# The end of a two-layer transformer kernel: first half's int8 product made with rows on partitions, scaled by ScalarE and transposed home; the last two tiles one by one; residual adds on GpSimd; four stores

## The chip, the cores and the metric

One Trainium2 chip; the kernel runs on one of its cores. The metric is the device time of one execution in microseconds, as the median of several runs. The engines are named as the profile names them: PE is TensorE (matmuls), DVE is VectorE, ACT is ScalarE, POOL is GpSimd, and SP issues most of the DMAs. PE writes into PSUM, which has eight banks here (`bank0` to `bank7`, each 128 partitions by 512 float32); POOL works on SBUF alone in this kernel.

## What is computed

Two pre-normalised transformer layers over `x` of shape (2, 512, 256), float32. Only the last block, the int8 layer of layer 1, is touched by the change:

```python
x = x + _L0_attn_ref(_layernorm(x), ...)
x = x + _L0_ffn_ref(_layernorm(x), ...)
x = x + _L1_attn_ref(_layernorm(x), ...)
x = x + _L1_ffn_ref(_layernorm(x), weight, bias)

def _L1_ffn_ref(x, weight, bias):
    w_scale = clip(max(abs(weight), axis=1), 1e-8) / 127
    w_q = clip(round(weight / w_scale), -128, 127)          # one scale per output row
    x_scale = maximum(max(abs(x), axis=2) / 127, 1e-12)     # one scale per token
    x_q = clip(round(x / x_scale), -128, 127)
    acc = einsum('bnd,od->bno', x_q, w_q)
    return acc * x_scale * w_scale + bias
```

## The kernel before

The 1024 tokens are eight tiles of 128 tokens (tokens on partitions, 256 features in the free dimension); tiles 0 to 3 are the first half, 4 to 7 the second. `X[:, t, :]` holds the residual stream of tile t. Every engine has its own instruction list, written out by hand, and the lists meet at semaphores. The attention of layer 1 runs as 32 windows, whose order on PE, ACT and DVE stands in three tables (`PE_ORDER`, `ACT_ORDER`, `DVE_ORDER`). The last window (`WINDOWS - 1`) holds the last attention products `A0`, `A1`, the last output projections `O0`, `O1`, and `I0`, `I1`, which are the int8 transposes and the int8 product of the first half. What follows the last window is straight code at the end of each engine's list.

The int8 layer works on a tile like this. DVE normalises it (`ln_statistics`, `ln_variance`, then POOL's `rstd`, then `ln_normalise`, which writes `XN`). POOL's `add_bias(6 or 7, qb_bc)` adds the output bias into `X`, so that the residual already holds it. DVE finds the largest magnitude of each token (`token_absmax`), its scale `xs` (`token_scale`) and the inverse (`token_inverse`), multiplies and clips at 127 (`clip_above`), and clips at -128 and rounds by adding a large constant (`clip_below`). ACT takes that constant off and writes bfloat16 (`quantised`), PE transposes the tile by a product with the identity (`int8_turn`), ACT copies the result out of PSUM (`int8_turned`, into `XQT`), and PE multiplies by the quantised weights `wqT` (`int8_product`). The product has tokens on partitions and the 256 outputs in the free dimension, so the token's scale `xs` is a number per partition, and the weight's scale is a row, spread over all partitions in `ws_bc`.

There are three groups (`GROUPS`): tiles 0 to 3, 4 to 5, and 6 to 7. For the first group ACT multiplies the product by `xs` on its way out of PSUM (`scale_tokens`), POOL multiplies by `ws_bc`, and DVE adds the residual (`finish(0)`). For the other two DVE does both products in one instruction (`dequantise`, L1554) and adds the residual (`finish`, L1561). One store for each group leaves on SP's queue: 512 KB, 256 KB and 256 KB.

The order after the last window: DVE does the statistics of tiles 4 and 5, then of 6 and 7, with the quantisation of tiles 4 and 5 between them, then the quantisation of 6 and 7, and after all of that `finish(0)`, `dequantise(1)`, `finish(1)`, `dequantise(2)`, `finish(2)`. POOL does both `rstd(7, ...)`, then the four products with `ws_bc`, then four `add_bias(7, ...)`. PE does `int8_turn` and `int8_product` of tiles 4 and 5, then of 6 and 7.

Of the kernel before, what the change touches and what calls it, by code (L numbers as in the profile page):

```python
# [18 lines left out]
ALU = mybir.AluOpType  # L19
# [41 lines left out]
def build(nc, x, wq0, wk0, wv0, fcT, fcb, wupT, wgateT, wdownT, pack1, bias_all, bo1, qw, qb, out):  # L61
    ctx = ExitStack()
    with ctx:
# [171 lines left out]
        y_scaled, y_weighted = sem("y_scaled"), sem("y_weighted")  # L235
# [163 lines left out]
        def _(sp):  # L399
# [59 lines left out]
            stores = ((y_done, CT, *GROUPS[0]), (y_done, CT + 2, *GROUPS[1]), (y_done, TILES, *GROUPS[2]))  # L459
            for ready, count, t0, t1 in stores:  # L460
                sp.wait_ge(ready, count)
# [7 lines left out]
        def _(pe):  # L469
# [281 lines left out]
            def int8_product(t0, t1):  # L751

                for t in range(t0, t1):
                    pe.wait_ge(qt_done, CT if t < CT else t + 1)
                    if t >= 2:
                        pe.wait_ge(y_scaled, min(t - 1, CT))
# [3 lines left out]
                    mm.then_inc(y_psum, 1)  # L760

            def window(w):
                p = PAIR_OF[w // 2]
                for kind, c in window_work("pe", w):
# [27 lines left out]
                    elif kind == "I":  # L792
                        int8_product(0, CT)
# [25 lines left out]
        def _(act):  # L819
# [170 lines left out]
            def scale_tokens():  # L990

                act.wait_ge(q_scale, 1)
                for t in range(CT):
                    act.wait_ge(y_psum, t + 1)
                    act.activation(OUT[:, t, :], bank[Y_BANKS[t]][:, 0:D], ACT.Copy,
                                   scale=xs[:, t:t + 1]).then_inc(y_scaled, 1)

            def window(w):
                p = PAIR_OF[w // 2]
                for kind, c in window_work("act", w):  # L1000
# [20 lines left out]
                    elif kind == "I":  # L1021
                        scale_tokens()
# [3 lines left out]
            for g in (1, 2):  # L1026
                quantised(g)
                int8_turned(g)
# [3 lines left out]
        def _(pool):  # L1032
# [117 lines left out]
            rstd(7, 0, 2)  # L1150
            rstd(7, 2, CT)

            for t in range(CT):
                pool.wait_ge(y_scaled, t + 1)
                pool.tensor_tensor(OUT[:, t, :], OUT[:, t, :], ws_bc[:], ALU.mult).then_inc(y_weighted, 1)
            add_bias(7, qb_bc, 0, 2)
# [515 lines left out]
```

## Time and profile before

| | us |
|---|---|
| median of 3 runs (512.42 to 512.47) | 512.46 |
| the profiled execution, its own time | 512.32 |
| span of the profiled execution, first to last instruction | 510.5 |
| its busy time: PE, DVE, ACT, POOL | 485.2, 383.0, 294.2, 282.9 |

The profiled execution took 1.8 us more than its span, and the median of the runs is 0.14 us above it. PE is busy for 95% of the span, but that is a mean over the whole program: the end, from about 494 us, is another stage, in which the engines pass four tiles from hand to hand. All times below count from the start of the span. The rows of a timeline merge consecutive instructions of one kind: `x2` with 0.74 us is the time from the start of the first to the end of the second.

### The profile page before, as it was taken

To read this page: it belongs to the slowest core of one execution; us is meant where nothing else is said; L and a number is where in the kernel's file an instruction comes from. 1 tells how busy PE (TensorE), PEld (TensorE's weight loads), DVE (VectorE), ACT (ScalarE), POOL (GpSimd) and SP (SyncE) were. 2 spreads that over 40 slices of the span, in tenths; PEclk is the share of its full clock that TensorE was granted. 3 is DMA by queue.
4 is the path that set the end of the run, shared out by engine and by line. 5 is a ranking of instruction groups with operands and counts; after the bars stand their busy time and mean duration, and the time that the engine had idled before them with its cause. 6 is when DMAs were issued, how large, how long until landed. Compare 5 with 4: busy or idle time off the path is not lost.

```text
span 510.5 us, 8907 instructions
## 1 busy us (share of the span) xinstructions
PE 485.2 (95%) x3016; PEld 432.3 (85%) x3016; DVE 383.0 (75%) x969; ACT 294.2 (58%) x690; POOL 282.9 (55%) x379
## 2 busy tenths in 40 slices
PE   8999999999999978899999999999999999999962
PEld 7888999899888856799889989999989989999851
DVE  2676786765755578788878778888879886678897
ACT  2356436535454646676666666766756757555652
POOL 1344234422655456786767677777767695512344
PEclk9999999999999999999999999999999999999995
DMA  8900000000010016564765665665664654000002
GB/s 278 379 14 2 1 0 1 0 1 1 24 41 1 0 52 179 161 177 131 199 170 154 189 168 155 187 168 146 196 173 129 196 153 126 1 1 1 1 1 82
DMA packets 54364, 51.58 MB, mean 101 GB/s; under 512 B 3504, under 2 KB 49712, under 8 KB 54320
## 3 DMA queue, kind: packets, MB, share of 16 engines
q1 hardware_dynamic: 53232, 49.98, 34.2%
q10 hardware_dynamic: 1088, 1.05, 0.6%
q8 instruction: 24, 0.39, 0.3%
q14 instruction: 20, 0.16, 0.1%
HBM read 32.92 MB, written 18.09 MB: 100 GB/s over the span
## 4 chain that ended last, share of the span: by engine, by line
PE 76%; DVE 11%; DMA 5%; ACT 3%; POOL 2%; issue 2%; SPq 1%; DVEq 0%; ACTq 0%
PE bank L390 19%; PE bank L392 18%; PE bank L391 18%; PE bank L610 3%; PE bank L611 3%; PE bank L682 2%; PE bank L683 2%; PE bank L681 2%; DMA Wv_sb<-wv 2%; DMA MV<-turned_dram 2%; PE bank L621 2%; PE bank L623 2%; DMA turned_dram<-BT 1%; DVE SM L1448 1%; DVE BT L1467 1%
## 5 line engine op out<-in xcount | busy, mean ns | idle before, releaser
L1120 POOL TENSOR_TENSOR PT_lo<-MV,PT_hi 128x512 fp32r<-128x512 f32 (+1 forms) x104 | 91.3, 909 | 51.5 <-ACT PT_hi L943 51.2
L932 ACT ACTIVATE PR<-SM,nmax 128x128 f32<-128x128 f32 (+3 forms) x128 | 72.0, 563 | 64.3 <-DVE nmax L1448 63.1
L1065 POOL TENSOR_TENSOR E_lo<-E,E_hi 128x512 fp32r<-128x512 f32 x24 | 31.0, 1297 | 54.6 <-ACT E_hi L856 47.5
L1448 DVE CUSTOM_DVE_ANT_0 SM<-bank,causal 128x384 f32<-128x384 f32 (+3 forms) x102 | 54.0, 530 | 9.3 <-PE bank L683 6.7
L390 PE MATMUL bank<-XT_hi,W_hi 128*128 128x512 f32 x128 | 52.4, 409 | 5.3 <-DVE V_lo L1430 3.8
L1467 DVE STREAM_TRANSPOSE BT<-PR 128x128 f32<-128x128 f32 (+1 forms) x104 | 48.1, 492 | 5.6 <-POOL PR L1104 3.6
L943 ACT CAST PT_hi<-MV 128x512 fp32r<-128x512 f32 (+1 forms) x104 | 42.1, 454 | 17.3 <-DMA MV<-turned_dram 17.1
L392 PE MATMUL bank<-XT_hi,W_lo 128*128 128x512 f32 x128 | 50.6, 395 | 0.0
L391 PE MATMUL bank<-XT_lo,W_hi 128*128 128x512 f32 x128 | 50.4, 394 | 0.0
L391 PE MATMUL bank<-PT_lo,V_hi 128*128 128x128 f32 (+3 forms) x130 | 41.6, 320 | 0.0
L392 PE MATMUL bank<-PT_hi,V_lo 128*128 128x128 f32 (+3 forms) x130 | 41.6, 320 | 0.0
L390 PE MATMUL bank<-PT_hi,V_hi 128*128 128x128 f32 (+3 forms) x130 | 40.4, 311 | 0.8 <-POOL PT_lo L1120 0.6
L851 ACT ACTIVATE E<-bank,nmax 128x512 f32<-128x512 f32 x24 | 16.5, 687 | 42.2 <-DVE nmax L1250 42.1
L390 PE MATMUL bank<-WO_hi,Z_hi 128*128 128x256 f32 x128 | 35.9, 280 | 1.9 <-DVE Z_lo L1482 1.9
L390 PE MATMUL bank<-W_hi,XT_hi 128*128 128x256 f32 x128 | 36.2, 283 | 1.5 <-DVE Q_lo L1433 1.2
L392 PE MATMUL bank<-WO_hi,Z_lo 128*128 128x256 f32 x128 | 35.8, 280 | 0.0
L392 PE MATMUL bank<-W_hi,XT_lo 128*128 128x256 f32 x128 | 35.8, 280 | 0.0
L391 PE MATMUL bank<-W_lo,XT_hi 128*128 128x256 f32 x128 | 35.7, 279 | 0.0
L391 PE MATMUL bank<-WO_lo,Z_hi 128*128 128x256 f32 x128 | 35.7, 279 | 0.0
L1433 DVE SCALAR_TENSOR_TENSOR Q_lo<-bank,bias,Q_hi 128x512 fp32r<-128x512 f32 x32 | 24.0, 750 | 15.1 <-ACT Q_hi L926 14.9
L949 ACT ACTIVATE Z_hi<-bank,bias 128x512 fp32r<-128x512 f32 x31 | 21.3, 688 | 23.6 <-PE bank L392 23.6
L681 PE MATMUL bank<-K_parts,Q_hi 128*128 128x384 f32 (+3 forms) x102 | 34.8, 342 | 0.0
(177 smaller groups left out, 1609.0 us busy)
## 6 DMA issues: line engine op xcount, KB each, us to landing
MV<-turned_dram SPq DMA_DIRECT2D x104, 160.0 KB, 3.2
turned_dram<-BT SPq DMA_DIRECT2D x26, 384.0 KB, 2.9
stage<-pack SPq DMA_DIRECT2D x32, 256.0 KB, 3.9
turned_dram<-BT SPq DMA_DIRECT2D x26, 256.0 KB, 3.2
X<-x SPq DMA_DIRECT2D x2, 512.0 KB, 8.8
wraw<-wupT SPq DMA_DIRECT2D x1, 1024.0 KB, 9.7
wraw<-wgateT SPq DMA_DIRECT2D x1, 1024.0 KB, 11.4
wraw<-wdownT SPq DMA_DIRECT2D x1, 1024.0 KB, 13.7
```

What stands on the lines that cost most here:

```text
L390: pe.matmul(dst, a_hi, b_hi, start=first, stop=False, skip_group_check=share)
L391: pe.matmul(dst, a_hi, b_lo, start=False, stop=False, skip_group_check=share)
L392: return pe.matmul(dst, a_lo, b_hi, start=False, stop=last, skip_group_check=share)
L681: pe.matmul(dst[:, 0:n], Q_hi[:, slot, cols], K_hi[:, slot, 0:n], start=True, stop=False)
L932: act.activation(PR[:, c, 0:(c + 1) * P], SM[:, c % 2, 0:(c + 1) * P], ACT.Exp, bias=nmax1[:, c:c + 1], scale=-1.0, accum_out=sum1[:, c:c ...
L943: act.copy(by_quad(PT_hi[w % 2], c), moved_part(w, c)).then_inc(mv_hi, 1)
L949: act.activation(Z_hi[g % 2][:, h, :], bank[6][:], ACT.Identity, bias=bias1[:, p, 4 + h:5 + h], scale=1.0).then_inc(z_hi, 1)
L1065: pool.tensor_tensor(E0_lo[:, m, :], E0[:, m, :], E0_hi[:, m, :], ALU.subtract).then_inc(e0_lo, 1)
L1120: pool.tensor_tensor(by_quad(PT_lo[w % 2], c), moved_part(w, c), by_quad(PT_hi[w % 2], c), ALU.subtract).then_inc(mv_lo, 1)
L1433: ins = dve.scalar_tensor_tensor(lo[:, w % 2, :], src, bias1[:, p, 2 * which + h:2 * which + h + 1], hi[:, w % 2, :], ALU.add, ALU.subtract)
L1448: dve.tensor_tensor_reduce(SM[:, c % 2, 0:n], s_bank(w, c)[:, 0:n], mask, 1.0, HIGHEST, ALU.add, ALU.min, nmax1[:, c:c + 1]).then_inc(s_ma ...
L1467: dve.transpose(BT[w % 2][:, :, moved_blocks(c), :].rearrange("p j b c -> p b j c"), PR[:, c, 0:(c + 1) * P].rearrange("p (b j c) -> p b j ...
```

## The change

On the first half, `int8_product(0, CT)` is replaced by `int8_product_turned`: the weights are the stationary operand and the four tiles the moving one, so the product has the 256 output rows on partitions (two banks of 128 rows) and 512 tokens in the free dimension. The weight's scale `qws` is then a number per partition, and ACT multiplies by it on the way out of PSUM (`scale_rows`, two instructions of 128x512 into `SM`, in place of `scale_tokens`, four of 128x256). PE transposes the eight 128x128 blocks back (`product_home`, float32, banks 2 and 3), and DVE does the rest of a tile in one instruction that multiplies by `xs` and adds `X` (`finish_home`). POOL's four products with `ws_bc` and the first `finish` are gone.

Tiles 6 and 7 are rounded one by one (`clip_last`), and ACT and PE pass them on one by one. POOL adds the residual of tiles 4, 5 and 6 after DVE's `dequantise`; DVE adds that of tile 7 (`finish_last`). POOL's two `add_bias(7, ...)` are moved: the first ahead of the second `rstd`, the second behind DVE's last rounding (`q_round` at 4). On DVE the output addition and the statistics of tiles 6 and 7 go ahead of the quantisation of tiles 4 and 5. There are four stores, of two tiles each.

```diff
-        Y_BANKS = (1, 0, 1, 0, 2, 1, 3, 0)
+        Y_BANKS = {CT: 7, CT + 1: 5, CT + 2: 0, CT + 3: 1}
-            k = (0, 1, 6, 4)[t // 2]
+            k = 6 if t == TILES - 1 else (0, 1, 6, 4)[t // 2]
...
-            stores = ((y_done, CT, *GROUPS[0]), (y_done, CT + 2, *GROUPS[1]), (y_done, TILES, *GROUPS[2]))
+            stores = (((y_done, 2), ), ((y_done, CT), ), ((y_added, 2), ), ((y_added, 3), (y_done, CT + 1)))
...
+            def int8_product_turned():
+                pe.wait_ge(qt_done, CT)
+                for o in range(KD):
+                    for k in range(KD):
+                        mm = pe.matmul(bank[o][:].rearrange("p (t n) -> p t n", n=P), wqT[:, k, o * P:(o + 1) * P],
+                                       XQT[:, 0:CT, k, :], start=(k == 0), stop=(k == KD - 1))
+                    mm.then_inc(yt_psum, 1)
+            def product_home():
+                for o in range(KD):
+                    pe.wait_ge(y_scaled, o + 1)
+                    for t in range(CT):
+                        at = t % 2 * D + o * P
+                        mm = pe.transpose(bank[2 + t // 2][:, at:at + P], SM[:, o, t * P:(t + 1) * P], ident[:])
+                mm.then_inc(y_home, 1)
...
-            def scale_tokens():
-                act.wait_ge(q_scale, 1)
-                for t in range(CT):
-                    act.wait_ge(y_psum, t + 1)
-                    act.activation(OUT[:, t, :], bank[Y_BANKS[t]][:, 0:D], ACT.Copy,
-                                   scale=xs[:, t:t + 1]).then_inc(y_scaled, 1)
+            def scale_rows():
+                for o in range(KD):
+                    act.wait_ge(yt_psum, o + 1)
+                    act.activation(SM[:, o, :], bank[o][:], ACT.Copy, scale=qws[:, o:o + 1]).then_inc(y_scaled, 1)
...
-            for g in (1, 2):
-                quantised(g)
-                int8_turned(g)
+            quantised(1)
+            int8_turned(1)
+            for t in range(TILES - 2, TILES):
+                act.wait_ge(q_round, t - 3)
+                act.activation(XQ_b[:, t, :], XQ2[:, t % CT, :], ACT.Copy, bias=-ROUND, scale=1.0).then_inc(q_ready, 1)
+            for t in range(TILES - 2, TILES):
+                act.wait_ge(qt_psum, t + 1)
+                act.copy(XQT[:, t, :, :].rearrange("p k n -> p (k n)"), q_bank(t)).then_inc(qt_done, 1)
...
+            def finish_home(t):
+                dve.wait_ge(y_home, 1)
+                dve.wait_ge(x_biased, 2 * TILES + t + 1)
+                dve.scalar_tensor_tensor(OUT[:, t, :], bank[2 + t // 2][:, t % 2 * D:(t % 2 + 1) * D], xs[:, t:t + 1],
+                                         X[:, t, :], ALU.mult, ALU.add).then_inc(y_done, 1)
...
-            clip_above(2)
-            clip_below(2)
-            finish(0)
+            for t in range(TILES - 2, TILES):
+                clip_last(t)
             for g in (1, 2):
+                finish_home(2 * g - 2)
+                finish_home(2 * g - 1)
                 dequantise(g)
-                finish(g)
+            finish_last()
```

What the tables and lists make of it on the engines is shown at three places. Line numbers of the changed kernel are shifted (its L1543 is L1519 of before, L1549 is L1525, L1201 is L1177, L1079 is L1056, L1071 is L1048).

DVE, second half, before: from the statistics of tiles 6 and 7 (`ln_ve`) through the quantisation of both pairs. `XQ1` is the clipped tile, `XQ2` the rounded one.

```order
L1171 TENSOR_SCALAR ln_ve<-ln_mv 128x2 [waits ln_aggr]
L1538 TENSOR_SCALAR XQ1<-XN,xinv 128x256 [waits q_round,q_inv]
L1538 TENSOR_SCALAR XQ1<-XN,xinv 128x256
L1177 TENSOR_SCALAR XN<-X,ln_mv,ln_rs 128x256 [waits ln_rstd]
L1177 TENSOR_SCALAR XN<-X,ln_mv,ln_rs 128x256
L1548 TENSOR_SCALAR XQ2<-XQ1 128x512 [waits q_ready,q_clip]
L1519 TENSOR_REDUCE xam<-XN 128x2 [waits ln_norm]
L1525 TENSOR_SCALAR xs<-xam 128x2 [waits q_absmax]
L1530 RECIPROCAL xinv<-xs 128x2 [waits q_scale]
L1538 TENSOR_SCALAR XQ1<-XN,xinv 128x256 [waits q_inv]
L1538 TENSOR_SCALAR XQ1<-XN,xinv 128x256
L1548 TENSOR_SCALAR XQ2<-XQ1 128x512 [waits q_clip]
```

The same place in the changed kernel, from `ln_normalise` of tiles 6 and 7 on:

```order
L1201 TENSOR_SCALAR XN<-X,ln_mv,ln_rs 128x256 [waits ln_rstd]
L1201 TENSOR_SCALAR XN<-X,ln_mv,ln_rs 128x256
L1562 TENSOR_SCALAR XQ1<-XN,xinv 128x256 [waits q_round,q_inv]
L1562 TENSOR_SCALAR XQ1<-XN,xinv 128x256
L1543 TENSOR_REDUCE xam<-XN 128x2 [waits ln_norm]
L1572 TENSOR_SCALAR XQ2<-XQ1 128x512 [waits q_ready,q_clip]
L1549 TENSOR_SCALAR xs<-xam 128x2 [waits q_absmax]
L1554 RECIPROCAL xinv<-xs 128x2 [waits q_scale]
L1577 TENSOR_SCALAR XQ1<-XN,xinv 128x256 [waits q_inv]
L1580 TENSOR_SCALAR XQ2<-XQ1 128x256 [waits q_clip]
L1577 TENSOR_SCALAR XQ1<-XN,xinv 128x256 [waits q_inv]
L1580 TENSOR_SCALAR XQ2<-XQ1 128x256 [waits q_clip]
```

The clipping of tiles 4 and 5 has moved behind `ln_normalise` of 6 and 7, the reduction of 6 and 7 ahead of the rounding of 4 and 5, and the last two tiles are clipped and rounded in four instructions.

POOL, the end of its list, before (`ln_rs` is the inverse deviation, `qb_bc` the bias, `ws_bc` the weight's scales):

```order
L1048 TENSOR_TENSOR ln_rs<-ln_ve,neg_half 128x2 [waits ln_var] x2
L1155 TENSOR_TENSOR OUT<-OUT,ws_bc 128x256 [waits y_scaled] x4
L1056 TENSOR_TENSOR X<-X,qb_bc 128x256 [waits ln_norm]
L1056 TENSOR_TENSOR X<-X,qb_bc 128x256
L1056 TENSOR_TENSOR X<-X,qb_bc 128x256 [waits ln_norm]
```

and in the changed kernel:

```order
L1071 TENSOR_TENSOR ln_rs<-ln_ve,neg_half 128x2 [waits ln_var]
L1079 TENSOR_TENSOR X<-X,qb_bc 128x256 [waits ln_norm]
L1079 TENSOR_TENSOR X<-X,qb_bc 128x256
L1071 TENSOR_TENSOR ln_rs<-ln_ve,neg_half 128x2 [waits ln_var]
L1079 TENSOR_TENSOR X<-X,qb_bc 128x256 [waits ln_norm,q_round]
L1181 TENSOR_TENSOR OUT<-OUT,X 128x256 [waits x_biased,y_product] x3
```

The four products are gone; two of the bias additions stand between the two `ln_rs`, two wait for DVE's last rounding, and three residual additions follow them.

DVE, the end of its list, before:

```order
L1561 TENSOR_TENSOR OUT<-OUT,X 128x256 [waits x_biased,y_weighted] x4
L1554 SCALAR_TENSOR_TENSOR OUT<-bank2,xs,ws_bc 128x256 [waits y_psum]
L1554 SCALAR_TENSOR_TENSOR OUT<-bank1,xs,ws_bc 128x256 [waits y_psum]
L1561 TENSOR_TENSOR OUT<-OUT,X 128x256 [waits x_biased,y_product] x2
L1554 SCALAR_TENSOR_TENSOR OUT<-bank3,xs,ws_bc 128x256 [waits y_psum]
L1554 SCALAR_TENSOR_TENSOR OUT<-bank0,xs,ws_bc 128x256 [waits y_psum]
```

and in the changed kernel:

```order
L1592 SCALAR_TENSOR_TENSOR OUT<-bank2,xs,X 128x256 [waits x_biased,y_home] x2
L1586 SCALAR_TENSOR_TENSOR OUT<-bank7,xs,ws_bc 128x256 [waits y_psum]
L1586 SCALAR_TENSOR_TENSOR OUT<-bank5,xs,ws_bc 128x256 [waits y_psum]
L1592 SCALAR_TENSOR_TENSOR OUT<-bank3,xs,X 128x256 [waits x_biased,y_home] x2
L1586 SCALAR_TENSOR_TENSOR OUT<-bank0,xs,ws_bc 128x256 [waits y_psum]
L1586 SCALAR_TENSOR_TENSOR OUT<-bank1,xs,ws_bc 128x256 [waits y_psum]
L1599 TENSOR_TENSOR OUT<-OUT,X 128x256 [waits x_biased,y_product]
```

All but the last instruction now read one operand from PSUM; the two halves of the first half's finishing stand around the `dequantise` of tiles 4 and 5, and of eight residual additions by themselves one is left on DVE.

## Rows read from the trace of the kernel before

**Rows 1.** Stretches: us, then busy us of PE, PEld, DVE, ACT, POOL; PEclk, DMA share.

```profile
497.70:499.90 2.20, 0.00 (x0) 0.00 (x0) 2.20 (x4) 0.45 (x2) 2.20 (x4) 1.00 0.00 0
...
500.00:510.50 10.50, 3.28 (x16) 1.55 (x16) 7.79 (x18) 2.41 (x4) 3.30 (x5) 0.50 0.29 100
```

**Rows 2.** Timeline of DVE: start us, us, engine, line, operation, tiles, count.

```profile
493.30 0.74 DVE L1177 TENSOR_SCALAR XN<-X,ln_mv,ln_rs 128x256 f32<-128x256 f32 x2
494.07 0.69 DVE L1519 TENSOR_REDUCE xam<-XN 128x2 f32<-128x512 f32 x1
494.67 0.68 DVE L1488 TENSOR_TENSOR X<-bank,X 128x512 f32<-128x512 f32 x1
...
495.39 0.75 DVE L1164 BATCH_NORM_STATS2 ln_st<-X 128x6 f32<-128x256 f32 x2
...
496.46 0.17 DVE L1171 TENSOR_SCALAR ln_ve<-ln_mv 128x2 f32<-128x2 f32 x1
496.54 0.62 DVE L1538 TENSOR_SCALAR XQ<-XN,xinv 128x256 f32<-128x256 f32 x2
497.48 1.54 DVE L1177 TENSOR_SCALAR XN<-X,ln_mv,ln_rs 128x256 f32<-128x256 f32 x2 [0.33 <-POOL ln_rs L1048]
498.94 0.94 DVE L1548 TENSOR_SCALAR XQ<-XQ 128x512 f32<-128x512 f32 x1
...
500.52 0.67 DVE L1525 TENSOR_SCALAR xs<-xam 128x2 f32<-128x2 f32 x1
...
502.76 0.83 DVE L1548 TENSOR_SCALAR XQ<-XQ 128x512 f32<-128x512 f32 x1
503.51 1.42 DVE L1561 TENSOR_TENSOR OUT<-OUT,X 128x256 f32<-128x256 f32 x4
504.85 0.86 DVE L1554 SCALAR_TENSOR_TENSOR OUT<-bank,xs,ws_bc 128x256 f32<-128x256 f32 x2
...
506.35 0.91 DVE L1554 SCALAR_TENSOR_TENSOR OUT<-bank,xs,ws_bc 128x256 f32<-128x256 f32 x2
507.18 0.75 DVE L1561 TENSOR_TENSOR OUT<-OUT,X 128x256 f32<-128x256 f32 x2
```

**Rows 3.** Timeline of POOL, its last nine instructions.

```profile
496.71 0.74 POOL L1048 TENSOR_TENSOR ln_rs<-ln_ve,neg_half 128x2 f32<-128x2 f32 x1 [3.44 <-DVE ln_ve L1171]
497.42 3.05 POOL L1155 TENSOR_TENSOR OUT<-OUT,ws_bc 128x256 f32<-128x256 f32 x4
500.44 2.86 POOL L1056 TENSOR_TENSOR X<-X,qb_bc 128x256 f32<-128x256 f32 x4
```

**Rows 4.** Timelines of PE and ACT: last projection, first product, last pair's three steps.

```profile
494.05 0.28 PE L392 MATMUL bank<-WO_hi,Z_lo 128*128 128x256 f32 x1
...
495.79 0.61 PE L758 MATMUL bank<-wqT,XQT 128*128 128x256 bf16 x4 [0.87 <-ACT XQT L971]
...
504.37 0.61 PE L748 MATMUL bank<-ident_b,XQ_b 128*128 128x128 bf16 x4 [1.32 <-ACT XQ_b L965]
...
505.07 0.58 ACT L971 COPY XQT<-bank 128x512 bf16<-128x512 bf16 x1 [0.76 <-PE bank L748]
505.71 1.03 PE L758 MATMUL bank<-wqT,XQT 128*128 128x256 bf16 x4 [0.73 <-ACT XQT L971]
```

**Rows 5.** Groups by form from 484 us: busy us, mean ns of one, idle before.

```profile
L692 PE MATMUL bank<-ident,PR 128*128 128x128 f32 x7 | 1.1, 280 | 0.6 <-DVE PT_lo L1459 0.6
...
L937 ACT CAST PT_hi<-bank 128x256 fp32r<-128x256 f32 x1 | 0.4, 372 | 0.0
```

**Rows 6.** Line L1494 (ns min/median/max of one), and POOL's timeline beside it.

```profile
L1494 DVE SCALAR_TENSOR_TENSOR X<-bank,gdscale,X x2: 476/476/477, 174.8 to 175.2; 128x256 f32<-128x256 f32 x2
...
174.96 1.42 POOL L1140 TENSOR_TENSOR X<-OUT,X 128x256 f32<-128x256 f32 x2 [2.36 <-ACT OUT L979]
```

**Rows 7.** Timelines of DVE and POOL at one L1371.

```profile
238.25 0.83 DVE L1371 SCALAR_TENSOR_TENSOR W_lo<-stage,W_hi 128x512 fp32r<-128x512 f32 x1
...
237.16 1.38 POOL L1120 TENSOR_TENSOR PT_lo<-MV,PT_hi 128x256 fp32r<-128x256 f32 x2
```

More of the change, by code:

```diff
@@ L234, in build @@
         q_ready, qt_psum, qt_done, y_psum = (sem(n) for n in ("q_ready", "qt_psum", "qt_done", "y_psum"))
-        y_scaled, y_weighted = sem("y_scaled"), sem("y_weighted")
+        yt_psum, y_scaled, y_home, y_added = sem("yt_psum"), sem("y_scaled"), sem("y_home"), sem("y_added")
         y_product = sem("y_product")
@@ L456, in _ @@
                     load_part(q + 1, 3)
-            stores = ((y_done, CT, *GROUPS[0]), (y_done, CT + 2, *GROUPS[1]), (y_done, TILES, *GROUPS[2]))
-            for ready, count, t0, t1 in stores:
-                sp.wait_ge(ready, count)
+            stores = (((y_done, 2), ), ((y_done, CT), ), ((y_added, 2), ), ((y_added, 3), (y_done, CT + 1)))
+            for i, ready in enumerate(stores):
+                t0, t1 = 2 * i, 2 * i + 2
+                for signal, count in ready:
+                    sp.wait_ge(signal, count)
                 rows = slice(t0 % CT * P, (t0 % CT + t1 - t0) * P)
@@ L753, in int8_product @@
                 for t in range(t0, t1):
-                    pe.wait_ge(qt_done, CT if t < CT else t + 1)
-                    if t >= 2:
-                        pe.wait_ge(y_scaled, min(t - 1, CT))
+                    pe.wait_ge(qt_done, t + 1)
+                    pe.wait_ge(y_scaled, KD)
                     for k in range(KD):
@@ L792, in window @@
                     elif kind == "I":
-                        int8_product(0, CT)
+                        int8_product_turned()
+                        product_home()
             pe.wait_ge(wa_dve, 1)
@@ L1021, in window @@
                     elif kind == "I":
[L1022 removed]
+                        scale_rows()
             for w in range(WINDOWS):
                 window(w)
[L1026 to L1028 removed]
+            quantised(1)
[6 more added lines that the diff above has]
+                act.copy(XQT[:, t, :, :].rearrange("p k n -> p (k n)"), q_bank(t)).then_inc(qt_done, 1)
         @block.gpsimd
@@ L1150, in _ @@
             rstd(7, 0, 2)
+            add_bias(7, qb_bc, 0, 2)
             rstd(7, 2, CT)
[L1153 to L1156, printed above, removed]
+            pool.wait_ge(q_round, 4)
             add_bias(7, qb_bc, 2, CT)
+            for t in range(CT, TILES - 1):
+                pool.wait_ge(y_product, t + 1 - CT)
+                pool.wait_ge(x_biased, 2 * TILES + t + 1)
+                pool.tensor_tensor(OUT[:, t, :], OUT[:, t, :], X[:, t, :], ALU.add).then_inc(y_added, 1)
         @block.vector
```

29 lines of the change are left out of this document (18 added, 11 removed).

## The prediction

> **What bounds the kernel now.** I read the chain of waits first: nearly all of the program hangs on PE, but its last stretch is DVE's, so the end is a stage of its own. The table by stretches shows the same: from 497.7 to 499.9 DVE and POOL are busy for all of 2.20 us and PE does nothing; PE's granted clock is 1.00 there and 0.50 from 500.0 on [rows 1]. Then I read DVE's timeline. From 497.48 to 507.93 it runs without a gap that matters [rows 2], the last store leaves right behind it, and the span ends at 510.5, 2.57 us later. The time of the kernel is therefore DVE's end plus a constant, as long as that store keeps its size (it does, 256 KB).
>
> DVE's own rows show why the stretch is long. `ln_normalise` took 0.74 us for two tiles at 493.30 and 1.54 at 497.48; a scale over 128x2 took 0.67 at 500.52, where the like-sized `ln_ve` took 0.17 [rows 2]. The slow ones lie inside POOL's 3.05 and 2.86 us of work, from 497.42 to 503.30 [rows 3]. Instructions that read PSUM keep their times: two instructions with a PSUM operand and `X` took 0.476 us each beside POOL's additions [rows 6].
>
> How I add durations: a DVE instruction that needs nothing new starts some 0.08 us before the one ahead of it ends (504.85 against 503.51 + 1.42), one that needs the result just made 0.04 after. Two additions take 0.75 and four 1.42, so each further one 0.34 [rows 2].
>
> **The change, DVE up to the last rounding.** Tiles 4 and 5 are normalised by 494.04, as before. The output addition of tiles 6 and 7 no longer stands behind the reduction; it waits for PE, which ends at 494.33 [rows 4]. So 494.37 + 0.68 = 495.05; statistics 0.04 + 0.75, to 495.84; from their end to the end of `ln_ve` it was 496.14 to 496.63, 0.49, which gives 496.33, 0.30 earlier. POOL's `ln_rs` follows by 0.08 + 0.74 [rows 3], 497.15. Meanwhile DVE does the reduction (0.69), the scale (0.17) and the inverse (as small, an estimate of 0.15), to 497.30. POOL's two bias additions that now stand ahead of this `ln_rs` run from 494.12 to 495.55 (2.86 / 4 = 0.72 each), done 0.8 before it is asked for, beside an addition from PSUM and the statistics. Whether POOL holds up statistics no row here shows; held until 495.55 they would come 0.46 later, which I keep for the range, since they have one operand.
>
> The product with `ws_bc` is gone from POOL, and its other bias additions wait for the last rounding: from 497.15 to 501.1 POOL does nothing. So DVE runs at its quick rates: `ln_normalise` 0.74 to 497.97 (before 499.02); clipping of 4 and 5, 0.62, to 498.51; reduction to 499.12; rounding of 4 and 5 no dearer than the 0.62 of two instructions over as many columns, I take 0.45, to 499.49 (before 499.88); scale and inverse to 499.77; then two times clip and round of one tile, (0.62 + 0.08) / 2 = 0.35 and about 0.30, with waits of 0.04: to 501.11. Before, that point was 502.76 + 0.83 = 503.59. This is the core of the gain: **2.48 us**.
>
> **Tiles 4 to 7 on ACT and PE.** From the last rounding to the product's start took 503.59 to 505.71, 2.12 us; the first tile reached DVE 0.64 after that start, the second 1.07 (the second product of the pair at 506.35 started at 506.78) [rows 2, 4]. So tiles 4 and 5: product at 499.49 + 2.12 = 501.61, DVE at 502.25 and 502.68. Tile 6 is rounded long before, but its transposes stand on PE behind this product, which holds PE 0.43 a tile: 502.47. Two transposes take 0.61 - 0.21 = 0.40, ACT starts 0.09 later, and copies 256 columns in place of 512: between the 0.37 of a copy of that size out of PSUM [rows 5] and the old 0.58 [rows 4]; I take 0.37, since it has the size. 503.33, PE 0.06 later, DVE at 504.03 for tile 6 and 504.46 for tile 7.
>
> **The first half.** All of it lies beside that. The turned product starts at 495.79 as before; its columns number 2048, as before, so at worst, at the lower clock, it costs twice 1.03 us. ACT's two passes over 512 columns of PSUM are like its copies of 0.58 each, and the eight float32 transposes 0.28 each, one at a time [rows 4, 5]. Even in line that is 495.79 + 2.06 + 1.16 + 2.24 = 501.25, and by overlaps and the clock of 1.00 nearer 498.5; DVE asks at 501.03 (`finish_home` is next on its list), and on PE the transposes of tile 4, queued behind `product_home`, are due at 499.49 + 504.37 - 503.59 = 500.27. Costed at nothing; without that cover all that stands behind on the two lists moves by what is late, at most 1.0.
>
> **DVE's and POOL's end.** `finish_home` of tiles 0 and 1 costs what `dequantise` does, 0.86 a pair, 501.03 to 501.89. `dequantise` of 4 waits until 502.25, of 5 until 502.68, to 503.16. Tiles 2 and 3, to 503.94. Tile 6, 504.03 to 504.51; tile 7, to 504.94. POOL: bias to 502.6, tile 4 from 502.81, tile 5 to 504.24, tile 6 from 504.59 to 505.31. The last addition on DVE could start at 504.98. It has two SBUF operands; such an instruction, L1371, started at 238.25 under POOL, whose work ended at 238.54, and ended 0.54 after that, for 512 columns [rows 7]. So I let it wait for POOL: 505.31 + 0.28 = **505.59**; unhindered it would be 505.39. Against 507.93 the end moves by 2.34 us.
>
> The row of a POOL addition (0.72) against one of DVE (0.34) speaks against the three that move [rows 2, 3]. The Trainium skill, GPSIMD Engine Reference, section 4.1 Engine selection, says so as a rule: elementwise additions belong on VectorE, since GpSimd is about twice as slow with two inputs. With the three on DVE, 1.02 us of work, of which its waits of 0.36 and 0.09 take up 0.45, the end would be some 0.5 later, 506.1, and the kernel 510.6; so by these rows moving them pays, because POOL has nothing else left, though each costs double.
>
> **The sum.** The profiled execution's 512.32 - 2.34 = 509.98; the median of the runs lies 0.14 above that execution, so 510.1. Bounds of the unknown: the copy at 0.58, +0.2; POOL's last addition at the 0.76 of a product with `ws_bc` (3.05 / 4), or somewhat over it, up to +0.2; clip and round dearer by half, +0.3; statistics, +0.4; last addition not held, -0.2. Not all come together: 509.9 to 510.8.
>
> **Rivals.** One: the clock. It stayed at 1.00 through 2.20 us without PE work and was 0.50 from 500.0 on [rows 1]; now PE is at work until about 498.5 and idle 1.8 until 500.3. If it stays at 1.00, the product of four matmuls takes 0.61 in place of 1.03 [rows 4], and DVE never waits: tile 6 done at 501.89 + 5 x 0.39 = 503.84, POOL at 504.64, DVE at 504.92, which gives **509.5**. For it speaks the shorter pause, against it that the work ahead is thin. Two: the stores. Before, the last two left about 1.6 us apart (506.35, as DVE turns to the last pair, and 507.93); now the third leaves at 504.3 right behind the second, and the fourth 1.3 later. Queued until the third has landed, 504.3 + 2.57, it would be 1.3 late; partly overlapped, as stores were before, or with ACT and PE at their upper bounds, 0.8: **510.9**. Three: the slow DVE rows are not POOL's doing. Then `ln_normalise`, rounding, scale and clipping keep 0.80 + 0.49 + 0.50 and the last pair some 0.5, and POOL's list is made shorter for nothing: **512.4**. Against it stand the quick rows of the same instructions with POOL idle. Four, slower: from 501.1 on POOL's five and DVE's nine instructions exclude one another, as L1371 was. Then they add: 5 x 0.76 + 9 x 0.39 and 14 hand-overs of 0.08 after 501.11 make 509.5, 1.6 after the old end, **514.1**. It decides only if a PSUM operand does not protect; the 0.476 beside POOL [rows 6] says it does, and an overlap of a fifth already brings the end back to the old one.
>
> **How the numbers follow.** Forecast 0.65; clock 0.14; stores 0.08; no lifting 0.08; exclusion 0.05. A measurement can tell 0.2% here, 1.0 us. Faster than that: 0.65 + 0.14 + 0.08 = 0.87; same 0.08; slower 0.05. The range takes the forecast's bounds, the clock and the stores: 509.3 to 511.1, leaving out 0.13.
>
> **What would show it.** `ln_normalise` at 0.74 near 497.2; the last rounding ending near 501.1; `y_home` there before DVE asks; `finish_home` at 0.48 beside POOL; tile 6's product behind 4 and 5's on PE; a last addition that lasts until POOL's end; the store's issue near 505.6. Wrong if POOL is busy between 497.2 and 501.1, if DVE idles at 501 for the transposes, or if instructions with a PSUM operand stretch beside POOL.

## The result, and the profile after

| | runs | median us | lowest to highest |
|---|---|---|---|
| before, beside it | 7 | 512.46 | 511.95 to 514.55 |
| after | 7 | 509.99 | 508.62 to 510.95 |

The ratio is 0.9936 with a 95% interval of 0.9912 to 0.9960, which on 512.46 is 509.18 us (507.95 to 510.41). The two medians lie closer, 2.47 us apart. Three of the seven runs of before are those of the table ahead of the prediction (512.42 to 512.47); the other four have a mean of 513.12, against which after's mean of 509.88 is 0.9937. A second comparison of the same two kernels (`a2_after_again`, below; 12 runs against 17) gave 0.9949 [0.9930, 0.9967], 509.85 on 512.46. The change makes the kernel faster by 0.5 to 0.65%. By these ratios the forecast of 510.1 is too high by 0.25 to 0.9 us; the first lies 0.12 us below the low end of its range, 509.3, the second inside it, and the intervals of both hold the forecast (they end at 510.41 and 510.77).

The profiled execution of after took 510.84 us, its span is 509.0 us. The end is read against one mark that both kernels have, the end of the normalisation of tiles 4 and 5: 494.04 before (493.30 + 0.74) [rows 2], 495.50 after (494.76 + 0.74). From there to DVE's last instruction, which I call the tail, it took 13.90 us before and 10.87 after (506.37 - 495.50). So the tail became 3.03 us shorter where 2.34 were forecast. The end of the span follows DVE's end by 2.66 (before 2.57).

Timeline of DVE in after (start us, us, engine, line, operation, tiles, shape, count, and in brackets the idle time before it and what ended it); it answers to [rows 2]:

```profile
494.76 0.74 DVE L1201 TENSOR_SCALAR XN<-X,ln_mv,ln_rs 128x256 f32<-128x256 f32 x2
495.83 0.69 DVE L1512 TENSOR_TENSOR X<-bank,X 128x512 f32<-128x512 f32 x1 [0.34 <-PE bank L392]
496.56 0.75 DVE L1188 BATCH_NORM_STATS2 ln_st<-X 128x6 f32<-128x256 f32 x2
...
498.73 0.71 DVE L1201 TENSOR_SCALAR XN<-X,ln_mv,ln_rs 128x256 f32<-128x256 f32 x2
499.36 0.61 DVE L1562 TENSOR_SCALAR XQ<-XN,xinv 128x256 f32<-128x256 f32 x2
499.88 0.68 DVE L1543 TENSOR_REDUCE xam<-XN 128x2 f32<-128x512 f32 x1
500.48 0.41 DVE L1572 TENSOR_SCALAR XQ<-XQ 128x512 f32<-128x512 f32 x1
500.81 0.16 DVE L1549 TENSOR_SCALAR xs<-xam 128x2 f32<-128x2 f32 x1
...
502.18 0.29 DVE L1580 TENSOR_SCALAR XQ<-XQ 128x256 f32<-128x256 f32 x1
502.39 0.87 DVE L1592 SCALAR_TENSOR_TENSOR OUT<-bank,xs,X 128x256 f32<-128x256 f32 x2
503.23 0.88 DVE L1586 SCALAR_TENSOR_TENSOR OUT<-bank,xs,ws_bc 128x256 f32<-128x256 f32 x2
504.02 0.87 DVE L1592 SCALAR_TENSOR_TENSOR OUT<-bank,xs,X 128x256 f32<-128x256 f32 x2
504.81 0.87 DVE L1586 SCALAR_TENSOR_TENSOR OUT<-bank,xs,ws_bc 128x256 f32<-128x256 f32 x2
505.71 0.66 DVE L1599 TENSOR_TENSOR OUT<-OUT,X 128x256 f32<-128x256 f32 x1
```

Two things are to be seen. Up to the last rounding (502.18 + 0.29 = 502.47) every instruction runs at its quick rate: the normalisation 0.71 where it was 1.54, the scale over 128x2 0.16 where it was 0.67. And from there on no row has a wait in brackets: the nine last instructions follow one another without a gap. The forecast had two waits there, for tile 4's and tile 6's products.

Timeline of POOL in after, from the same place on, which answers to [rows 3]:

```profile
495.58 1.41 POOL L1079 TENSOR_TENSOR X<-X,qb_bc 128x256 f32<-128x256 f32 x2 [0.85 <-DVE XN L1201]
497.88 0.71 POOL L1071 TENSOR_TENSOR ln_rs<-ln_ve,neg_half 128x2 f32<-128x2 f32 x1 [0.89 <-DVE ln_ve L1195]
502.55 1.41 POOL L1079 TENSOR_TENSOR X<-X,qb_bc 128x256 f32<-128x256 f32 x2 [3.97 <-DVE XQ L1580]
503.92 2.17 POOL L1181 TENSOR_TENSOR OUT<-OUT,X 128x256 f32<-128x256 f32 x3
```

POOL does nothing for 3.97 us, in which DVE quantises. Then its five additions run back to back, to 506.09 (503.92 + 2.17), and DVE's last addition ends 0.28 after that.

Timelines of PE, ACT and SP in after (PE and ACT answer to [rows 4]):

```profile
498.64 1.23 PE L778 MATMUL bank<-ident,SM 128*128 128x128 f32 x8 [0.35 <-ACT SM L1014]
501.67 0.40 PE L750 MATMUL bank<-ident_b,XQ_b 128*128 128x128 bf16 x4 [1.79 <-ACT XQ_b L985]
502.80 0.61 PE L759 MATMUL bank<-wqT,XQT 128*128 128x256 bf16 x4 [0.73 <-ACT XQT L991]
503.25 0.46 PE L750 MATMUL bank<-ident_b,XQ_b 128*128 128x128 bf16 x4
503.99 0.86 PE L759 MATMUL bank<-wqT,XQT 128*128 128x256 bf16 x4 [0.28 <-ACT XQT L1051]
...
497.90 1.27 ACT L1014 ACTIVATE SM<-bank,qws 128x512 f32<-128x512 f32 x2 [0.70 <-PE bank L768]
...
503.28 3.53 SPq L465 DMA_DIRECT2D out<-OUT  x4
```

The four matmuls of tiles 4 and 5 took 0.61 us (before 1.03 for the last pair), the eight transposes home were done at 499.87, 2.5 us before DVE asks for them at 502.39, and the stores' issues are spread over 3.53 us.

Stretches of after (us, busy us of PE, PEld, DVE, ACT, POOL, then PE's granted clock, DMA share, GB/s), against [rows 1]:

```profile
499.90:502.00 2.10, 0.33 (x4) 0.23 (x4) 2.00 (x8) 0.63 (x1) 0.00 (x0) 1.00 0.00 0
502.70:504.30 1.60, 1.22 (x11) 0.77 (x12) 1.60 (x5) 1.32 (x5) 1.60 (x3) 1.00 0.04 13
504.32:509.00 4.68, 0.53 (x3) 0.05 (x2) 2.01 (x5) 0.00 (x0) 1.73 (x3) 0.50 0.63 217
```

Granted 1.00 is the level of 2.4 GHz, 0.50 that of 1.2 GHz. Before, the clock fell at 499.93, 5.9 us after the mark. Here it holds until 504.32, 8.8 after the mark, while the last tiles' product runs.

All that lies ahead of the mark is the same code, yet it ended 1.47 us later in this profile. The profiles' groups of the line that waits for the window data out of DRAM show where (busy us, mean ns, idle before, releaser). Before:

```profile
L943 ACT CAST PT_hi<-MV 128x512 fp32r<-128x512 f32 (+1 forms) x104 | 42.1, 454 | 17.3 <-DMA MV<-turned_dram 17.1
```

The same group after, with its line number there:

```profile
L963 ACT CAST PT_hi<-MV 128x512 fp32r<-128x512 f32 (+1 forms) x104 | 42.3, 456 | 18.8 <-DMA MV<-turned_dram 18.6
```

ACT's wait for these loads grew by 1.5 us. In the other profiles of this study, with the same code ahead of it, the mark lies between 492.52 and 494.45. That is about the size of the difference between these two profiles, but the loads are not shown to be the whole cause: in f8_two_on_dve (below) this wait was 20.1 us, and its mark came at 494.33. In any case the execution of after that was profiled was a late one, and a single execution's time tells little of an end that changed by 3 us; the tail does.

### The profile page after: what moved, and what is told of

It reads as the page before. It is cut to its first block, busy times and chain, and to the rows that moved or that the text cites. A ratio compares the mean times of both kernels' runs of the same rounds, so it can differ in the third digit from the quotient of the medians.

```text
span 509.0 us, 8910 instructions
## 1 busy us (share of the span) xinstructions
PE 485.7 (95%) x3020; PEld 433.0 (85%) x3020; DVE 379.8 (75%) x967; ACT 294.7 (58%) x690; POOL 282.1 (55%) x378
## 4 chain that ended last, share of the span: by engine, by line
PE 65%; DMA 11%; DVE 11%; ACT 4%; POOL 3%; issue 2%; SPq 2%; DVEq 0%; ACTq 0%
PE bank L390 16%; PE bank L392 16%; PE bank L391 16%; DMA MV<-turned_dram 5%; DMA turned_dram<-BT 4%; PE bank L612 3%; PE bank L613 3%; PE bank L685 2%; PE bank L684 2%; PE bank L683 2%; DMA Wv_sb<-wv 2%; PE bank L623 2%; PE bank L625 2%; DVE SM L1472 1%; POOL PT_lo L1143 1%
## 6 DMA issues: line engine op xcount, KB each, us to landing
wraw<-wgateT SPq DMA_DIRECT2D x1, 1024.0 KB, 11.8
```

## The experiments

In the table "tail" is the time from the mark to DVE's end, "rounding" from the mark to the end of the last rounding, "rest" their difference; then when the granted clock fell, from the mark. Times are the profiled executions', one for each row; the two of after agree within 0.01 us.

| kernel | rounding | rest | tail | clock falls |
|---|---|---|---|---|
| before | 9.55 | 4.35 | 13.90 | 5.9 |
| forecast for after | 7.07 | 4.48 | 11.55 | (low) |
| after | 6.97 | 3.89 | 10.87 | 8.8 |
| a2_after_again | 6.98 | 3.89 | 10.87 | 8.8 |
| e2_filler | 7.01 | 3.89 | 10.90 | 10.2 |
| e1_one_home | 6.97 | 4.26 | 11.23 | 6.8 |
| e4_bias_early | 7.45 | 4.47 | 11.91 | 6.4 |
| e5_pool_load | 8.68 | 4.46 | 13.14 | 5.9 |
| f7_pair | 6.78 | 4.17 | 10.96 | 11.0 |
| f8_two_on_dve | 6.98 | 3.87 | 10.84 | 11.8 |
| f6_adds_on_dve | 6.98 | 4.54 | 11.52 | 11.9 |
| f9_old_product | 7.01 | 5.96 | 12.96 | 11.3 |
| e10_act_round | 6.36 | 3.83 | 10.19 | 7.6 |
| e3_before_filler | 9.56 | 4.25 | 13.81 | 13.3 |

**The clock: e1_one_home and e2_filler.** Two theories stood for the 0.69 us by which the tail is shorter than forecast: the transposes home keep PE's clock up, or the work after the last rounding is simply cheaper than I priced it. In e1 seven of eight transposes are left out (the output of the first half is then not the product); in e2 six matmuls of 512 columns, whose results nobody uses, follow the transposes.

```
-                    for t in range(CT):
+                    for t in () if o < KD - 1 else (CT - 1,):
```

> The changed kernel with seven of the eight transposes home left out (tiles 0 to 2 and half of tile 3 are then not the product). PE has 0.3 us of work in its pause instead of 1.2. The end is measured from the end of the normalisation of tiles 4 and 5 to DVE's last instruction: 13.90 us before, 10.87 after. Theory of the clock: the end beat the forecast (11.55) because PE's clock stayed at 1.00 to 504.3; with less work it falls before the transposes of tiles 4 and 5, their product takes 1.03 instead of 0.61, DVE waits 0.3 to 0.5 at dequantise, and the end is 11.4 to 11.6. Rival, DVE's terms were mis-sized and the clock is without effect: 10.8 to 10.9 at either clock. If the clock does not fall, both say 10.9 and the run tells nothing.

```
...
                         product_home()
+                        filler(6)
```

> The changed kernel with six more matmuls of 512 columns (1.3 us, their result is not used) on PE behind the transposes home, in its pause. Theory of the clock: the clock stays at 1.00 to the last product or nearly, the end is 10.8 to 10.9 us, and DVE runs through its nine last instructions without a wait over 0.1. Rival, the clock is without effect: the same end, but then the kernel with one transpose must give it too at a clock of 0.50.

Measured: e2's tail is 10.90, as after's. Its time is 509.78 us (4 runs), 0.9941 [0.9917, 0.9964]. e1's is 11.23, and its time 510.12 (9 runs), 0.9951 [0.9937, 0.9966]; the two intervals overlap, so it is the tails that tell them apart. Stretches of e1 (columns as above):

```profile
498.79:500.55 1.76, 0.00 (x0) 0.00 (x0) 1.66 (x7) 0.63 (x1) 0.00 (x0) 1.00 0.00 0
500.56:501.15 0.59, 0.39 (x4) 0.22 (x4) 0.56 (x3) 0.10 (x1) 0.00 (x0) 1.00 0.00 0
501.60:503.30 1.70, 1.46 (x8) 0.95 (x8) 1.51 (x5) 0.98 (x5) 1.65 (x3) 0.50 0.10 37
```

PE's timeline of e1 there:

```profile
498.19 0.30 PE L778 MATMUL bank<-ident,SM 128*128 128x128 f32 x1 [1.01 <-ACT SM L1014]
500.56 0.40 PE L750 MATMUL bank<-ident_b,XQ_b 128*128 128x128 bf16 x4 [2.06 <-ACT XQ_b L985]
501.69 1.04 PE L759 MATMUL bank<-wqT,XQT 128*128 128x256 bf16 x4 [0.73 <-ACT XQT L991]
```

And DVE's, at its first wait for it:

```profile
501.27 0.87 DVE L1592 SCALAR_TENSOR_TENSOR OUT<-bank,xs,X 128x256 f32<-128x256 f32 x2
502.33 0.91 DVE L1586 SCALAR_TENSOR_TENSOR OUT<-bank,xs,ws_bc 128x256 f32<-128x256 f32 x2 [0.19 <-PE bank L759]
```

With one transpose in place of eight the clock falls after tile 4's turn and before its product. The product takes 1.04 us in place of 0.61, and DVE's wait, absent in after, is back. The last rounding did not move (6.97 in both). So the clock is worth 0.37 us of the tail when it falls there; the 11.4 to 11.6 expected was for a fall ahead of the turn. In e4 and e5 below it falls still earlier, ahead of the turn of tile 4, and there the rest is 4.47 and 4.46: the forecast's 4.48. My prices after the last rounding were right for the low level, and the two levels differ by 0.58 us (4.47 - 3.89).

That the work in the pause matters is shown by the runs and not by one profile of each: the mean granted clock of a run was 0.990 to 0.993 in all nine of e1, 0.996 or 0.997 in all four of e2, and 0.994 or more in 11 of 19 of after. The other eight of after had 0.990 to 0.993, as e1 has. So the transposes make it likely that the clock stays up, and do not make it sure.

**POOL beside DVE: e4_bias_early and e5_pool_load.** e4 takes away the one wait that keeps POOL's bias additions behind the last rounding; e5 puts four products with `ws_bc` back beside the quantisation, on a tile that nobody reads.

```
             rstd(7, 2, CT)
-            pool.wait_ge(q_round, 4)
             add_bias(7, qb_bc, 2, CT)
```

> The changed kernel without POOL's wait for the last rounding, so that the second pair of bias additions (1.4 us) runs as soon as tiles 6 and 7 are normalised, beside DVE's clipping, scale and rounding. Theory of the forecast, POOL holds up DVE's SBUF instructions: the last rounding comes 0.5 to 0.9 later after the normalisation of tiles 4 and 5 than the 6.97 us of the changed kernel, and the end is 11.3 to 11.8 us. Rival, the slow rows of before were not POOL's doing: 6.97 and 10.87.

```
             rstd(7, 2, CT)
+            for c, at in ((1, 0), (2, 0), (3, 0), (3, D)):
+                pool.tensor_tensor(PR[:, c, at:at + D], PR[:, c, at:at + D], ws_bc[:], ALU.mult)
             pool.wait_ge(q_round, 4)
```

> The changed kernel with POOL's old load put back as mere cost: four products of 128x256 with ws_bc on scratch, behind the second ln_rs, where the old kernel had its four. Theory of the forecast: normalisation of tiles 6 and 7 takes 1.5 us instead of 0.71, clipping 1.3 instead of 0.6, the scale 0.6 instead of 0.16; the last rounding comes at 8.7 to 9.2 us instead of 6.97 and the end at 12.6 to 13.2 instead of 10.87. Rival, order alone makes the gain: 6.97 and 10.87.

Measured: the last rounding came 0.47 later in e4, a little less than expected, and 1.71 later in e5, at the low end of what was expected. The tails were 11.91 and 13.14; e4's is above its 11.3 to 11.8 because the clock fell as well. DVE's and POOL's timelines of e5:

```profile
497.22 1.45 DVE L1203 TENSOR_SCALAR XN<-X,ln_mv,ln_rs 128x256 f32<-128x256 f32 x2
498.59 1.54 DVE L1564 TENSOR_SCALAR XQ<-XN,xinv 128x256 f32<-128x256 f32 x2
500.05 0.67 DVE L1545 TENSOR_REDUCE xam<-XN 128x2 f32<-128x512 f32 x1
500.64 0.41 DVE L1574 TENSOR_SCALAR XQ<-XQ 128x512 f32<-128x512 f32 x1
...
497.05 2.93 POOL L1177 TENSOR_TENSOR PR<-PR,ws_bc 128x256 f32<-128x256 f32 x4
```

And of e4:

```profile
496.78 1.08 DVE L1561 TENSOR_SCALAR XQ<-XN,xinv 128x256 f32<-128x256 f32 x2
497.78 0.67 DVE L1542 TENSOR_REDUCE xam<-XN 128x2 f32<-128x512 f32 x1
498.37 0.41 DVE L1571 TENSOR_SCALAR XQ<-XQ 128x512 f32<-128x512 f32 x1
...
496.94 1.49 POOL L1079 TENSOR_TENSOR X<-X,qb_bc 128x256 f32<-128x256 f32 x2 [0.94 <-DVE XN L1200]
```

The instructions that POOL's work overlaps take two to two and a half times as long, 1.45 and 1.54 for 0.71 and 0.61; those after its end are quick again. The normalisation's 0.74 and the clipping's 0.93 are all but 0.04 of e5's 1.71. The reduction, one operand in and 128x2 out, is not touched in e4, though POOL's second addition lies beside it. So the third rival of the prediction (the slow rows are not POOL's doing) falls, and the core of the gain is shown by putting it back: 1.71 of the 2.58 us that the last rounding gained. The other 0.87 (the rest of what POOL did there before, and the new order of DVE's list) was not taken apart. e5's time was 511.51, e4's 509.29, one run each and thus without weight beside the 1 us by which runs differ.

PE's timeline of e5 and two stretches of it tell more of the clock:

```profile
497.13 1.24 PE L778 MATMUL bank<-ident,SM 128*128 128x128 f32 x8 [0.35 <-ACT SM L1014]
501.84 0.61 PE L750 MATMUL bank<-ident_b,XQ_b 128*128 128x128 bf16 x4 [3.46 <-ACT XQ_b L985]
```

```profile
498.38:499.86 1.48, 0.00 (x0) 0.00 (x0) 1.48 (x3) 0.00 (x0) 1.48 (x3) 1.00 0.00 0
499.90:501.80 1.90, 0.00 (x0) 0.00 (x0) 1.80 (x7) 0.63 (x1) 0.08 (x1) 0.50 0.00 0
```

It fell 5.9 us after the mark, 1.5 us into PE's pause. Up to there PE had done the same as in after, the eight transposes at the same distance from the mark, and after's clock held through the 1.79 us of its pause. So neither the length of the pause nor DVE's delay explains why it fell in e5.

**The parts of the tail, at the high clock.** The next four have the idle matmuls of e2, so that the clock is not part of the comparison; they are to be read against e2's tail of 10.90. f6 takes the three additions from POOL to DVE, f7 quantises tiles 6 and 7 as a pair, f8 leaves tile 6's addition to DVE, f9 makes the first half's product with tokens on partitions as before, but without ACT's scale: DVE does both its steps. Each ran once (509.35 to 509.95 us), so only the tails are compared.

```
-            for t in range(CT, TILES - 1):
-                pool.wait_ge(y_product, t + 1 - CT)
...
-            finish_last()
+                for t in range(*GROUPS[g]):
+                    finish_last(t)
...
```

> The kernel with the six filler matmuls (its end 10.90 us, clock up) with the residual additions of tiles 4, 5 and 6 put back on DVE; POOL's list ends with the bias additions. The prediction's weighing of GpSimd's slowness: DVE is the bound of the end, three additions of 0.34 more on it, less the 0.28 that the last addition no longer waits for POOL, so the end is 11.5 to 11.7. Rival, the rule that an addition on GpSimd costs double and gains nothing here: 10.9 or less.

```
-            for t in range(TILES - 2, TILES):
-                clip_last(t)
+            clip_above(2)
+            clip_below(2)
...
```

> The filler kernel with tiles 6 and 7 clipped, rounded, transposed and copied as a pair, as before. DVE's clipping and rounding get some 0.2 us shorter (last rounding at 6.75 to 6.85 after the normalisation of tiles 4 and 5 instead of 7.0), the pair's product reaches DVE later (DVE waits 0.2 to 0.3 before the last dequantise). Theory, DVE bounds the end: 10.8 to 11.0, one by one is worth nothing at the clock of 1.00. Rival, the hand-over of the last tiles bounds the end: 11.3 or more.

```
-            for t in range(CT, TILES - 1):
+            for t in range(CT, TILES - 2):
                 pool.wait_ge(y_product, t + 1 - CT)
...
-            finish_last()
+            for t in range(TILES - 2, TILES):
+                finish_last(t)
...
```

> The filler kernel with the residual additions of tiles 6 and 7 both on DVE, POOL adding those of tiles 4 and 5 alone. If the last addition is held up by POOL's (0.66 us instead of 0.41, as in the changed kernel), it is now free: two additions in 0.75 us, the end at 10.8 to 10.9, so that the wait cost as much as the addition that POOL took. Rival, no hold, the last addition is long for another reason: two additions of 0.6 and the end at 11.2 to 11.4.

```
...
-                        int8_product_turned()
-                        product_home()
+                        first_product()
+                        filler(12)
...
+                add_home(2 * g - 2)
+                add_home(2 * g - 1)
...
```

> The filler kernel (twelve matmuls) with the first half's product made as before, tokens on partitions, and without ACT's scaling and the transposes home: DVE multiplies by xs and ws_bc in one instruction and adds X in another, four additions more than the changed kernel. POOL stays out of it, so its products are not put back. Theory, DVE bounds the end and the turned product is worth the four additions that it folds away: 4 x 0.34, the end at 12.2 to 12.4. Rival, the first half has slack and the turned product is worth nothing: 10.9 to 11.1.

Measured, against 10.90: f6 +0.62, f7 +0.06, f8 -0.06, f9 +2.07 us. With the additions on DVE its list is 1.02 us longer and its end 0.62 later, so POOL, slower by the piece, is the better place here as long as it is idle. One tile at a time is worth next to nothing at this clock: the pair's rounding is done 0.23 earlier (6.78), and DVE then waits 0.16 for the first product. Whether POOL does three additions or two is even. f9 missed its 12.2 to 12.4: it cost 0.7 more than the 1.36 of four more additions at 0.34. DVE's timeline of f9 shows why:

```profile
500.23 1.28 DVE L1607 TENSOR_TENSOR OUT<-OUT,X 128x256 f32<-128x256 f32 x2
...
503.01 1.00 DVE L1607 TENSOR_TENSOR OUT<-OUT,X 128x256 f32<-128x256 f32 x2
```

Two such additions take 0.75 with POOL idle [rows 2]; beside POOL's bias and additions they take 1.28 and 1.00. The folded form that the change uses, L1592 with one operand in PSUM, took 0.87 a pair with POOL idle or busy. So a part of the turned product's worth is that it leaves DVE one addition with two SBUF operands in place of five.

**The old order at the high clock: e3_before_filler.** The kernel before, with 12 and 4 idle matmuls in its two pauses.

```
...
                         int8_product(0, CT)
+                        filler(12)
...
                 int8_product(*GROUPS[g])
+                if g == 1:
+                    filler(4)
```

> The kernel before with twelve idle matmuls behind the first half's product and four behind that of tiles 4 and 5 (their result is not used), so that the clock stays up. If the clock matters only where DVE waits for PE, it is worth next to nothing in the old order: the products take 0.61 to 0.75 us instead of 1.03 but DVE is busy till then, and the end is 13.7 to 13.9 instead of 13.90. Rival, the clock by itself is a part of the gain in any order: 13.2 to 13.5.

Measured (one run, 512.61 us): a tail of 13.81 against 13.90, with the clock at 1.00 through both products (0.61 each):

```profile
502.22 0.61 PE L758 MATMUL bank<-wqT,XQT 128*128 128x256 bf16 x4 [0.73 <-ACT XQT L979]
...
505.92 0.61 PE L758 MATMUL bank<-wqT,XQT 128*128 128x256 bf16 x4 [0.73 <-ACT XQT L979]
```

In the old order DVE was busy until the product came, so the clock was worth 0.09 there. Most of the gain of after is not the clock's; but the new order, whose DVE is sooner ready, pays up to 0.58 for a low one.

**Both kernels again, and a version beyond: a2_after_again and e10_act_round.** a2 is the changed kernel itself. In e10 ACT multiplies and rounds tiles 4 and 5 (a copy with scale `xinv` and the rounding constant as bias), and DVE's two instructions for that are gone; the clip to the int8 range is left out for these two tiles.

> The changed kernel as it is, timed again. Its first comparison gave a ratio of 0.9936, a gain of 3.3 us, more than the end gained in the two traces (13.90 to 10.87, 3.03 us), and the single runs of either kernel differ by 2 us. If that difference is the part ahead of the end, which the change does not touch, the gain is 2.3 to 3.0 us (0.9941 to 0.9955), nearer 2.5 where the clock falls early (mean granted clock 0.992 or less) and 3.0 where it falls late (0.994 or more). Rival, the change also makes the part ahead faster: 3.3 us again.

```
+            for t in (CT, CT + 1):
+                act.wait_ge(q_inv, 2)
+                act.wait_ge(ln_norm, CT * 7 + 2)
+                act.activation(XQ2[:, t % CT, :], XN[:, t % CT, :], ACT.Copy, bias=ROUND,
+                               scale=xinv[:, t:t + 1]).then_inc(q_act, 1)
...
-            clip_above(1)
             token_absmax(2)
-            clip_below(1)
```

> The changed kernel with tiles 4 and 5 multiplied and rounded on ScalarE (one pass with the token's inverse as scale and the rounding constant as bias) instead of clipped and rounded on DVE; the clipping is left out there, since the scaled values end at 127. If DVE bounds the end, 0.6 + 0.3 us come off its list: last rounding at 6.2 to 6.3 instead of 6.97, the end at 10.0 to 10.3 instead of 10.87, the kernel 0.6 to 0.8 faster than the changed one. Rival, the hand-over through ACT and PE bounds the end: 10.7 or more.

Measured: a2 509.52 us (12 runs, 507.14 to 511.19) beside 512.23 (17 runs of before), and a tail that agrees with the first profile's to 0.01. e10 509.11 (6 runs), 0.9937 [0.9913, 0.9961] against before. ACT's timeline of e10 has the new work:

```profile
496.90 0.90 ACT L1047 ACTIVATE XQ<-XN,xinv 128x256 f32<-128x256 f32 x2
497.89 0.63 ACT L1050 ACTIVATE XQ_b<-XQ 128x512 bf16<-128x512 f32 x1
```

The last rounding comes 0.62 earlier than in a2 (0.7 to 0.8 was expected) and the end 0.68: DVE really was the bound up to the last rounding, and ACT had room. e10 is the fastest by its median and its tail; against a2 the intervals of the times overlap, so by times alone it is not shown to be faster.

## Why the prediction was right, and where it was wrong

**What bounds the end: right.** DVE's list set it before and up to the last rounding after; e10 takes work off that list, and the last rounding comes 0.62 earlier, the end 0.68.

**Up to the last rounding: right.** Forecast 7.07 us after the mark, measured 6.97, a gain of 2.58 for 2.48. e5 puts POOL's four products back and loses 1.71 of it. The estimates stood near their rows: clipping 0.61 for 0.62, rounding 0.41 for 0.45, clip and round of one tile 0.35 and 0.29 for 0.35 and 0.30. The statistics beside POOL's bias additions took 0.75, as without them; the 0.46 kept for that was not needed.

**The first half at nothing: right**, with 2.5 us to spare. The fear that the float32 transposes go one at a time was too dark: eight took 1.23 where 2.24 were set down as the worst.

**The last addition on DVE: right.** It ended 0.28 after POOL's last, the figure that the forecast had drawn from L1371 [rows 7]; in f8, with POOL done before, two such additions took 0.75 us where the one of after took 0.66. **The stores: right.** Four issues lie within 3.53 us, and a store took 2.2 us from issue to landing by the median, the last among them (508.62 for an issue at 506.44); the second rival fell. **Full exclusion: fell too**: beside POOL the instructions with a PSUM operand took 0.87 a pair, as without it.

**The choice of the low clock: wrong.** This is the step that failed. The forecast took the level of before, 0.50 from 500.0 on [rows 1], for the end of after too, gave it 0.65, and left the clock that stays up 0.14, because "the work ahead is thin". The rows show it up until 504.32, and the rest after the last rounding is 3.89 us instead of 4.48. The rival's own end, 504.92, is 10.88 after the mark; measured 10.87. The mechanism of the rival was right to the step: product in 0.61, DVE never waits. What I could have weighed: before, PE had nothing at all for 3.03 us after the last product of the first half, and its clock was still at 1.00 through 2.20 us of that [rows 1]; in after that pause begins with eight transposes of 1.23 us, and 1.79 us are left. e1, with one transpose, shows that they matter: none of its nine runs has the mean clock of the eleven of after. They do not decide it alone: e4 and e5 have all eight and fell at 6.4 and 5.9 us, and eight runs of after itself have the mean clock of an early fall. What decides between the two from one execution to the next stays open. No row of before spoke for 0.14 rather than an even chance.

With the clock at the high level POOL's waits go as well, and its five additions of 0.72 fill the last 3.5 us beside DVE's list. That the two then end almost even is shown by f8 (-0.06).

**The size that follows.** By the profiles the tail gives 3.03 us at the high level and would give 2.45 at the low one (2.34 forecast, 0.10 more from the rounding). Over all 36 runs of before beside these kernels and 19 of after the medians are 512.39 and 509.60, 2.8 apart. Of the 19, 11 have a mean granted clock of 0.994 or more and a mean time of 509.36, the other 8, at 0.993 or less, 509.91. In the profiles a clock that held until the last tiles' product goes with 0.995 and more, one that fell early with 0.993 and less (e1, e4). So it seems that after has both ends, from one execution to the next, and the median lies between the forecast and its first rival. This is argued from the means: only two of the 19 were profiled, and both had the high one. By an estimate from these numbers, 11 of 19 executions with 0.58 more than 2.45 make 2.79, which is what all the runs together gave. Of the 0.45 us beyond the forecast's 2.34 the clock thus has 0.34 and the rounding 0.10. The 3.28 of the first ratio is 0.5 more still; no run shows a cause in the kernel for that, and it fits the spread of the runs: the four of before that have a mean of 513.12 lie 0.65 above the mean of all 36, 512.47.

**The range: wrong in one respect.** It was built from the costs of the end and took the part ahead as fixed, because three runs of before agreed within 0.05 us. The runs here spread by about 1.0 us (standard deviation, 36 of before and 19 of after), where from is shown above in part only; that is as much as the bounds of all the costs together. With seven runs a side the ratio's interval is 2.5 us wide. A low end at 508.8 would have held both comparisons.

**The weighing of the skill's rule: right in sign, somewhat small.** The Trainium skill, GPSIMD Engine Reference, section 4.1 Engine selection, puts elementwise additions on VectorE. Here f6 followed that and lost 0.62 us, where 0.5 was worked out at the low clock; one POOL addition took 0.72 against 0.34 to 0.37 on DVE, so the rule's factor of two agrees, and it is the free engine that decides.

## What to carry to other kernels

When an engine's instructions differ by a factor of two between like places, look at what its neighbour does at that time before shortening anything: taking POOL's work out of DVE's way (four products gone, four additions moved), together with a new order on DVE, gave 2.6 us, and putting four products back took 1.7. An order that makes one engine ready earlier makes another one's clock matter: price the products at both levels, and give both a fair chance where no row of before decides between them. Before setting a range on an edit worth 0.5%, know how much whole executions differ; three equal ones say little.

## What the runs showed of the hardware

The granted clock at the end went with PE's work in the pause, and not with that alone. With eight float32 transposes between the products it stayed at 1.00 until 8.8 us after the mark in both profiles of after, and the mean granted clock of 11 of its 19 runs was 0.994 or more; with one of them (e1) it fell at 6.8, and all nine runs had 0.990 to 0.993. With all eight it also fell at 6.4 (e4) and 5.9 (e5), there 1.5 us into a pause, though PE's work up to that point was that of after.

Whether POOL holds up DVE goes by the instruction and where its operands lie. Beside POOL's products a DVE `TENSOR_SCALAR` out of SBUF went from 0.61 to 1.54 us a pair (e5), and beside its additions an addition of two SBUF operands from 0.75 to 1.28 a pair (f9), while a reduction (0.67, e4) and instructions with one operand in PSUM (0.87 a pair) kept their times. The Trainium skill, SBUF — State Buffer, section Who interferes with whom, says that a DVE instruction with at most one SBUF input outside its 2-port modes does not contend with GpSimd, one with two does against reads; by that rule the slow `TENSOR_SCALAR` would be in a 2-port mode, which no run here shows by itself; the rest agrees with the rows just given. What surprised is the size on the smallest: the scale over 128x2 took 0.67 for 0.17 [rows 2], which would fit waiting out what is left of a POOL instruction of 0.72.
